# Second layer weights of six experts turned by DMA instead of TensorE in a macaron block on one Trainium2 core

## The reference

```python
def _swiglu(u, w1, w2, w3):                      # hidden size 341
    h = einsum('...d,hd->...h', u, w1); v = einsum('...d,hd->...h', u, w2)
    return einsum('...h,dh->...d', sigmoid(h) * h * v, w3)

def ffn(x):                                      # 8 routed experts, top 4, and a shared one
    gate = x @ Wg.T + routing_bias
    weights = softmax over the top 4 of gate, 0 elsewhere
    return _swiglu(x, Ws1, Ws2, Ws3) + sum_e weights[e] * _swiglu(x, W1[e], W2[e], W3[e])

x = x + 0.5 * ffn(layernorm(x))
x = x + attention(layernorm(x))                  # 16 heads of 64, causal, W_qkv and W_out
x = x + 0.5 * ffn(layernorm(x))                  # the same ffn weights
```

## Time and profile before

| | |
|---|---|
| median of three runs | 649.8 us |
| the profiled execution, in its own time | 649.4 us |
| its span, first to last instruction | 647.7 us |
| PE busy | 634.1 us (98%), 7870 products |
| DVE busy | 593.5 us (92%) |
| ACT busy | 562.2 us (87%) |
| POOL busy | 498.2 us (77%) |
| granted TensorE clock | 1.00 as the page lists it |
| chain that ended last | PE 88%, DVE 6%, issue 2%, ACT 2% |

### The profile page before, as it was taken

How to read it: one execution, slowest core, us unless ns; L and a number is a source line. 1 busy time by engine, 2 the same in 40 slices (tenths; PEclk the granted TensorE clock), 3 DMA queues, 4 the chain that set the end, 5 groups by cost and what they waited for, 6 DMA issues and landing times.

```text
span 647.7 us, 21027 instructions
## 1 busy us (share of the span) xinstructions
PE 634.1 (98%) x7870; PEld 419.4 (65%) x7870; DVE 593.5 (92%) x1655; ACT 562.2 (87%) x1108; POOL 498.2 (77%) x617
## 2 busy tenths in 40 slices
PE   6799999999999999999999999999999999999997
PEld 5466665666676566667657666756666676666666
DVE  4998799999999999999999999999999998888887
ACT  5989997999999799999889999998999996566554
POOL 3254785899899779799968988986799997665545
PEclk9999999999999999999999999999999999999999
DMA  7900000487789278796746777973698874200000
GB/s 202 285 2 2 3 1 2 84 146 133 129 123 169 42 124 140 126 136 120 128 70 122 140 137 127 148 132 63 107 137 147 140 138 78 50 18 2 18 1 18
DMA packets 226489, 62.97 MB, mean 97 GB/s; under 512 B 213202, under 2 KB 225620, under 8 KB 226388
## 3 DMA queue, kind: packets, MB, share of 16 engines
q1 hardware_dynamic: 226388, 61.64, 53.4%
HBM read 7.87 MB, written 1.05 MB: 14 GB/s over the span
## 4 chain that ended last, share of the span: by engine, by line
PE 88%; DVE 6%; issue 2%; ACT 2%; DMA 0%; POOL 0%; SPq 0%; DVEq 0%; POOLq 0%; ACTq 0%
PE bank L1164 25%; PE bank L1166 24%; PE bank L1165 24%; PE bank L1344 8%; PE bank L1307 5%; DVE probs L1842 2%; DVE glu L1750 1%; DVE xs L1781 1%; PE bank L1172 1%; DVE glu L1755 1%; PE bank L1208 1%; DMA bias_b<-in_L_ffn_routing_bias 0%; ACT gluh L1511 0%; ACT glu L1487 0%; POOL glul L1127 0%
## 5 line engine op out<-in xcount | busy, mean ns | idle before, releaser
L1127 POOL TENSOR_TENSOR glul<-glu,gluh 128x512 f16<-128x512 f32 x191 | 218.9, 1162 | 78.4 <-ACT gluh L1511 77.9
L1131 POOL TENSOR_TENSOR paired<-probs,paired 128x512 f16<-128x512 f32 x160 | 184.2, 1163 | 22.5 <-ACT paired L1536 21.6
L1490 ACT ACTIVATE glu<-bank,tanh_scale 128x512 f32<-128x512 f32 x167 | 112.4, 680 | 37.9 <-PE bank L1166 34.4
L1528 ACT ACTIVATE probs<-probs,exp_bias 128x128 f32<-128x128 f32 (+3 forms) x256 | 129.1, 552 | 4.2 <-POOL exp_bias L1139 4.1
L1842 DVE CUSTOM_DVE_ANT_0 probs<-bank,causal,score_scale 128x128 f32<-128x128 f32 (+3 forms) x256 | 126.2, 545 | 3.6 <-POOL paired L1131 2.9
L1164 PE MATMUL bank<-w3h,gluh 128*128 128x128 f16 x708 | 125.3, 219 | 0.1
L1166 PE MATMUL bank<-w3h,glul 128*128 128x128 f16 x708 | 125.1, 219 | 0.0
L1165 PE MATMUL bank<-w3l,gluh 128*128 128x128 f16 x708 | 125.1, 219 | 0.0
L1750 DVE SCALAR_TENSOR_TENSOR glu<-glu,bank 128x512 f32<-128x512 f32 x167 | 113.5, 679 | 9.6 <-ACT glu L1490 9.0
L1511 ACT ACTIVATE gluh<-glu 128x512 f16<-128x512 f32 x191 | 113.4, 623 | 9.6 <-DVE glu L1755 8.8
L1755 DVE SCALAR_TENSOR_TENSOR glu<-glu,bank 128x512 f32<-128x512 f32 x167 | 114.7, 687 | 5.8
(11 more groups left out here) (247 smaller groups left out, 1613.4 us busy)
## 6 DMA issues: line engine op xcount, KB each, us to landing
pT<-paired SPq DMA_TRANSPOSE x160, 3.3
attention_raw<-in_L_attn_W_qkv SPq DMA_DIRECT2D x6, 256.0 KB, 5.2
xs<-in_L_attn_inputs SPq DMA_DIRECT2D x4, 256.0 KB, 4.1
vh<-in_L_ffn_W SPq DMA_DIRECT2D x6, 128.0 KB
pT<-in_L_ffn_W SPq DMA_DIRECT2D x6, 128.0 KB
out<-xs SPq DMA_DIRECT2D x3, 256.0 KB, 2.8
raw_more<-in_L_ffn_W SPq DMA_DIRECT2D x4, 128.0 KB
attention_raw<-in_L_attn_W_out SPq DMA_DIRECT2D x2, 256.0 KB, 6.2
```

The lines of the kernel that those rows point to most:

```text
L1127: pool.tensor_tensor(glul[pair][:, :], g[:, :], gluh[pair][:, :], ALU.subtract).then_inc(glu_low)
L1131: pool.tensor_tensor(paired[n % PAIRED][:, 1, :], probs[n % PROBS][:, :], paired[n % PAIRED][:, 0, :], ALU.subtract).then_inc(probs_low)
L1490: act.activation(g[:, :], psum[b1.bank][:, :], ACT.Tanh, scale=tanh_scale[:, j:j + 1]).then_inc(tanh_made)
L1528: e = act.activation(pr[:, at:at + (qt + 1) * P], pr[:, at:at + (qt + 1) * P], ACT.Exp, bias=exp_bias[:, gp % 2, qt, head:head + 1], scale ...
```

## The change

w3 of the experts n = 3 to 8 no longer passes through TensorE and PSUM. POOL multiplies the raw weight by its scale in place (`scale_w3`), ACT copies it as float16 (`high_w3`), POOL subtracts (`low_w3`), both into `attn_pair`, a buffer that attention uses later, with the two halves of each part beside each other, and one DMA with transposition (`turn_w3`, on SP) brings both halves to their place; w3's high and low half are now two slices of one tensor for that. The step v of these experts only holds the bank that the transposition had, so that all others get the banks that they had. Products wait for the DMA (`drain_of`) instead of for DVE. `split_hidden`, `down` and all else are as before. Twelve unread products at the start become seven, five of which stand behind `norm_turn` and two behind the first `gate`. The order strings of all four engines are new; `Schedule` gives the same layers, shares and banks.

```diff
-WARMING = 12
+WARMING = 7
+TURNED_W3 = 3
@@ Schedule.turn_weights
-        if len(turned) == 3:
+        if len(turned) == (3 if n < TURNED_W3 else 2):
             self.raw_left[n] = use
@@ Schedule.prepare
+            if stage in "vr" and n >= TURNED_W3:
+                if stage == "v":
+                    self.spared[n] = self.free.popleft()
+                else:
+                    self.free.append(self.spared.pop(n))
+                    for kind in ("scale_w3", "high_w3", "low_w3", "turn_w3"):
+                        self.add(kind, n=n)
+                    self.weights_ready[n, 2] = TurnedW3(n)
+            elif stage in "tuv":
                 self.turn_weights(n, "tuv".index(stage))
@@ ORDER, two of its lines
-        "BFFFFFFFFFFFTTzFNTGTTSgNhhTGSTTTTThTddhhdhhGddShTTTddTdhhddTTdGhhShddTTTddTdhRhTdTXhhdzTdThhdTddghdh"
+        "BTzFFFFFTGNSgFFTTTNhhGSTTTTThdThdhhdhGddSTThTdddhhdTGddhdShhhTTTddddRhdThXddhzTTdhhhhdgddddhhhhhhhdd"
...
@@ macaron
-        w3h, w3l = sb("w3h", [P, len(PARTS), D], F16), sb("w3l", [P, len(PARTS), D], F16)
+        w3_pair = sb("w3", [P, len(PARTS), 2, D], F16)
+        w3h, w3l = w3_pair[:, :, 0, :], w3_pair[:, :, 1, :]
+        staged = lambda n: attn_pair[n % 2][:, :, :].rearrange("p a (j k) -> p (a j) k", k=D).rearrange("p (j a) k -> p j a k", a=2)[:, 0:len(TILES_OF[n])]
@@ sync
+                elif kind == "turn_w3":
+                    n = s["n"]
+                    q.wait_ge(w3_low, n - TURNED_W3 + 1)
+                    sp.dma_start_transpose(w3_pair[:, parts_of(n), :, :].rearrange("p j a d -> p (j a) d"),
+                                           staged(n).rearrange("p j a k -> p (j a k)")).then_inc(w3_turned[n % 2], 16)
@@ gpsimd
+                elif kind == "scale_w3":
+                    n = s["n"]
+                    raw = raw3[n % RAWS][:, 0:len(TILES_OF[n]) * P]
+                    q.wait_ge(scales_made, group_of(n) + 1)
+                    pool.tensor_scalar(raw, raw, scale_of(n, 4), None, ALU.mult).then_inc(w3_scaled)
+                elif kind == "low_w3":
+                    n = s["n"]
+                    raw = raw3[n % RAWS][:, 0:len(TILES_OF[n]) * P].rearrange("p (j k) -> p j k", k=P)
+                    q.wait_ge(w3_high, n - TURNED_W3 + 1)
+                    pool.tensor_tensor(staged(n)[:, :, 1, :], raw, staged(n)[:, :, 0, :], ALU.subtract).then_inc(w3_low)
@@ tensor, drain_of
+                if isinstance(use, TurnedW3):
+                    q.wait_ge(w3_turned[use.n % 2], 16 * ((use.n - TURNED_W3) // 2 + 1))
@@ scalar
+                elif kind == "high_w3":
+                    n = s["n"]
...
+                    q.wait_ge(w3_scaled, n - TURNED_W3 + 1)
+                    if n >= TURNED_W3 + 2:
+                        q.wait_ge(w3_turned[n % 2], 16 * ((n - TURNED_W3) // 2))
+                    act.activation(staged(n)[:, :, 0, :], raw, ACT.Copy).then_inc(w3_high)
```

More of the change, by code:

```diff
@@ L142 @@
 Turned = namedtuple("Turned", "n")
+TurnedW3 = namedtuple("TurnedW3", "n")
 class Schedule:
@@ new lines @@
+        "qkwwhwqwqhddwqhkwhwwxqxdqhhwwoqwwhdddwqqhwwhwhdwhdwhhwdwkwvvvwhxqxdvkhqqhddvhdkqdohwqqhvwwhwwqkdhwdq"
+        "qxghvwxwdwwqkdhdddwwqqhvhwwqkwhdwwdqqhhwwwxqxkhdwwqqhhddwwwqkdhdqqwwwhoqwhwddwqqhwwhxwhhxwdhdhwwdkwh"
+        "ddvvvvwwhqkhqqvhddxqxkhogwwhdwqqvhwddqwkhwwddqqhvhwwwqkhwddwqqhvwhwwxqxkhdwwqqhwdqwdwkhhwdwqqdwhwqkh"
+        "ddwwqqhwwxohwwqxhddwqqwhhddwwwhdhwhhwwdkvvwwhvvdqxghkxdqqhvhdddkqhowqqhdvwwhqwwkhwddqqxvwwhhwxqwkhwd"
+        "qqvdwhwwdwqkhddwqqhwhwwddqkhwwxqxqdwwhhwkqwhddwddqqwhhwoqwwdhqqwwhhdxwwwghhwxdddhhhddwwddwwhhhhhxhox"
@@ new lines @@
+        "rhsshhsshWhhssWsWsshhhWlWzhsskhsvvhvsvhshssskheeppsvehpeepkehppelhysvephpespkhseeppeuhspvehpeskpehpe"
+        "pusseevprhphsepepsskhepepusehpepkeheppesphsuepshepkheeppssuehphleypeephpusepespeshphhepsephhhsskssvv"
+        "vhusulvkheyepphssvhepeeppkehepspshevpheekpphepusseesprvhpseeppkhseupepshevphepepkhsseepsuphheepspekh"
+        "epupsephhespseekpephpuessphlepepyhepepsuehhpessphheepphhsssskhlyvvvuvhuskhepsehvpeeppkhssseeepprhpss"
+        "vehpepepkhepuessphevpheeppskheepsspuhevhpepepskheeppsuhespepepkhhespeupsehpseskphepepehuesplphysepep"
@@ new lines @@
+        "czhckhvvhvcvhhmkhmmvhmckhmmhvichmkhimcmhvihmkihmmgrvhjihcimkhmmchimkhimchmihmkhimnmhhicmaichmmihhich"
+        "hhnihkvvihvcmkhvmmhchvmckahmmhvihmkihmmgrjvchimikhcmmhvihmckhimmhihimkhcmmhhiimkcnhmmhcaimihnmmhhhci"
+        "ihhchikhcvvvivhmkhmmvhcmhkagrjhmmvihmickhmmhvichmkhimmhvhiimckhmmhciimkhhmmchimkhimnhminahmichmmchhi"
+        "ihchhhikvivhvvmgrjkhmmchvchmhkammhcivhmikhmmivhhcmikhmmcvhiimkhcmmnihhmkhimcmihhmikhcmmchhaimihmmhhi"
+        "iDDDDgrhjchhhiccihhhhhhahccnhhchhhhchhhhhccgrjhhhchhhhchchhhhchhhcchhhhhhccchhhhhHccclllllllllll"
@@ L893, in macaron @@
         first_gathered, first_spread = signal("first_gathered"), signal("first_spread")
+        w3_scaled, w3_high, w3_low = signal("w3_scaled"), signal("w3_high"), signal("w3_low")
+        w3_turned = [signal(f"w3_turned{i}") for i in range(2)]
         eps_made = signal("eps_made")
@@ L1154, in drain_of @@
             def drain_of(use):
-                q.wait_ge(drained[use.bank], use.n + use.d)
+                if isinstance(use, TurnedW3):
+                    q.wait_ge(w3_turned[use.n % 2], 16 * ((use.n - TURNED_W3) // 2 + 1))
+                else:
+                    q.wait_ge(drained[use.bank], use.n + use.d)
             def x_there(ready):
@@ L1398, in scalar @@
                     else:
-                        high_of(split, psum[split.use.bank][:, 0:len(TILES_OF[n]) * D],
-                                w3h[:, parts_of(n), :].rearrange("p j d -> p (j d)"), scale_of(n, 4))
+                        high_of(split, by_part(psum[split.use.bank], n),
+                                w3h[:, parts_of(n), :], scale_of(n, 4))
+                elif kind == "high_w3":
+                    n = s["n"]
+                    raw = raw3[n % RAWS][:, 0:len(TILES_OF[n]) * P].rearrange("p (j k) -> p j k", k=P)
+                    q.wait_ge(w3_scaled, n - TURNED_W3 + 1)
+                    if n >= TURNED_W3 + 2:
+                        q.wait_ge(w3_turned[n % 2], 16 * ((n - TURNED_W3) // 2))
+                    act.activation(staged(n)[:, :, 0, :], raw, ACT.Copy).then_inc(w3_high)
                 elif kind == "measure" and s["by"] == "A":
@@ L1661, in vector @@
                     else:
-                        high, low = (w[:, parts_of(n), :].rearrange("p j d -> p (j d)") for w in (w3h, w3l))
-                        low_of(split, psum[split.use.bank][:, 0:len(TILES_OF[n]) * D], high, low, scale_of(n, 4))
+                        high, low = (w[:, parts_of(n), :] for w in (w3h, w3l))
+                        low_of(split, by_part(psum[split.use.bank], n), high, low, scale_of(n, 4))
                 elif kind == "norm_stats":
```

47 lines of the change are left out of this document (16 added, 31 removed), and 2 rows, old and new, of the table KINDS.

## The result

The changed kernel takes 652.69 us (median of 12 runs, 650.99 to 654.76), the kernel before 649.84 (12 runs): ratio 1.0045, 95% interval 1.0034 to 1.0057. It is slower by 0.45%, 2.9 us; the forecast was 647.6 with a range up to 650.9. The profiled execution is the longest of the twelve (654.76 us, span 653.0), so its sizes are an upper end. The spread itself says something: the mean granted clock was 1.00 in three of the twelve runs, and these took 650.99, 651.13 and 651.59 us; it was 0.995 to 0.997 in seven (652.14 to 653.62) and 0.994 in two (654.63 and 654.76). So the kernel takes about 651.1 us at full clock, and the median lies 1.6 us above that, among runs with a lower clock.

What follows compares the result with a forecast made beforehand. PE bounds the first layer from 40 us, DVE and PE attention, PE the end. Gains of 2.0 us at the first projection, 0.2 from DVE's cushion, 0 behind: -2.2, median 647.6 us, range 645.9 to 650.9.

Steps and rivals of the forecast that it cites:

- The term for 18 to 40 us: Reordered `gather_max` and third silu free one copy's time before the tile at 26.09 us: gain 0.5 us, bounds 0 and 1.
- the port: Rival: small DVE steps of the scales blocked by POOL instructions, three more hits, 2.9 us less 0.5 slack: 650.0, chance 0.12.
- Half clock: Rival, at the start: native products at lower clock take 1.9 us longer; with POOL late 648.9 us, joint chance 0.12.
- Turnings, 2.2 us: First layer, PE: 20 w3 turnings removed at 0.11 us each; 17 lie in full PE time, gain 1.9 us.
- The start, +0.1 with bounds -0.5 and +1.9: Start: five unread products fewer bring nothing by themselves, since ACT's queue is late next; +0.1 us.
- POOL: Six subtractions 5.8 us and six scalings 5 us added; sum fits POOL's free time; arrives together with PE at first projection.
- The chain of POOL to the first projection: Before attention: last low half and 17 POOL instructions until 97.7 us, level with PE; taken as 98.0, gain 2.0.
- DVE and `expo`: Second router: `expo` 2.9 us earlier removes DVE's 3.55 us wait; DVE 2.2 us earlier at attention, counted as -0.2.
- DMAs and attention, 0: Six transposing w3 DMAs cost nothing, landing 3.3 us after issue; attention does the same work reordered, counted 0.
- The rival of the slower attention stage: Between 105 and 550 us the new order worsens DVE's queue, idle time above 17.1 us grows: 652.0 us, chance 0.18.

Runs made afterwards that it cites:

- splits_wait: Changed kernel, two groups of GpSimd low halves waiting for VectorE's scale_units, scaling of expert 3 put behind the first three low halves: 648.73 us, 0.9981 of the kernel before.
- warm12: Changed kernel with the five unread products put back at the head of TensorE's program, twelve instead of seven: 652.31 us, ratio 1.0029 to the kernel before.
- W3_alone: Kernel before, its orders and twelve unread products kept, only the w3 part for experts 3 to 8 changed, new operations placed by hand: 660.03 us, ratio 1.0156.

## Why the prediction was wrong, point by point

**The step that failed** is an overlap taken as free. The term for 18 to 40 us was a gain of 0.5, bounds 0 and 1, and POOL's additions between 40 and 60 us were free because "POOL is busy for 10.96 of 20". Both asked whether an engine has time, and neither asked what runs beside it. In their place the trace has PE gaps of 2.92 us (before 30.82) and 1.37 us (before 63.45) and a stretch of half clock behind each; all gaps of PE over 0.15 us from 24 to 70 us add up to 5.6 us, before to 0.9. The mechanism was in hand, as the rival called the port, from the earlier trace rows, and its price (three more hits, 2.9 us less 0.5 of slack) was nearly that of the first place alone (0.92 + 0.93 + 0.98 = 2.8 us over the times of before). It was given 0.12 because "it is one hit in four groups". That was a miscount in two ways. The trace before holds a second hit, a step of the scales on 15 columns at 50.87 us that takes 0.60 instead of 0.17. And the number of hits isn't a property of the chip that carries over, but of the two strings: the new one of DVE has `scale_units` ahead of two low halves, which the listings of the two orders tell without any run. In the trace after I count nine stretched small steps, 7.1 us in all over their normal time, against two with 1.4 us before. Seven of the nine stand beside low halves of tiles, which both kernels have; one, `spread` at 52.55 us with 0.98 instead of 0.22, beside a subtraction that the change added, and one beside an added scaling (0.47 instead of 0.24).

**Half clock** was the other rival that came true, at another place. It was expected at the native products, which took 2.40 us (the text named 2.5 as wrong), and cost 0.6 us at the start: with the data there at the same time (first turning at 7.42 and 7.45) the first low half is at 16.97 in splits_wait, with seven unread products, and at 16.39 in warm12, with twelve. In the changed kernel it is at 17.39, because the data landed 0.5 us later in this execution (first turning at 7.93). Behind the gaps at 27.9 and 62 us it cost more. At 2.4 GHz a product of 512 columns starts every 0.22 us, here every 0.42 us:

```profile
65.28 0.63 PE L1199 MATMUL bank<-xnT,w2h 128*128 128x512 f16 x1
65.70 0.63 PE L1200 MATMUL bank<-xnT,w2l 128*128 128x512 f16 x1
```

The clock of 0.83 on the mean of ten microseconds is 1.7 us of full clock lost in each of the two stretches. The profiled execution has two of them and lies 3.7 us over the 651.1 of full clock. The median lies 1.6 us over it, at 0.997, half of what that execution's 0.994 lacks, so it had one of them by that reckoning.

**Turnings, 2.2 us.** The number fits the bookkeeping. From 25 us on splits_wait has gaps of 0.61, 0.85, 0.59, 1.15 and 0.28 us, 3.5 in all, and the kernel before 0.24 and 0.67; yet at the 30th tile and at the last it is 0.2 us ahead, from 0.1 ahead at the second. So some 2.5 us of work are gone in between, near the 1.9 to 2.2 forecast (the two orders differ, so it is rough: at the 32nd tile it is 1.1 us behind). W3_alone won 1.3 to 1.7 us until it stalled. By itself the term is not shown.

**The start, +0.1 with bounds -0.5 and +1.9.** Measured +1.0 at the first low half and +0.3 at the second tile; inside the bounds. `spread0` came at 15.12 us, 1.1 later than worked out. ACT's queue was indeed what came late next (its first high half at 16.42, I had said 16.0).

**POOL.** The subtraction took 0.92 and 1.16 us, for 0.87 and 1.16. The scaling was mis-sized, outside my bounds of 0.52 and 1.16 for 512 columns:

```profile
L1105 POOL TENSOR_SCALAR paired<-paired,half_scale 128x384 f32<-128x384 f32 x2 | 2.5, 1253 | 16.1 <-DVE half_scale L1655 16.1
L1105 POOL TENSOR_SCALAR vl<-vl,half_scale 128x512 f32<-128x512 f32 x1 | 1.6, 1571 | 0.0
```

With one input tensor instead of two it is not shorter than the subtraction, but a third longer: 8.1 us for the six, where 5 were planned. The chain of POOL to the first projection did not decide: PE was full from 70 us on and got there at 107.07, 9 us behind the forecast of 98, with the last low half of n = 8 at 84.39. Since PE came so late, this is no test of how long POOL's chain is.

**DVE and `expo`.** ACT's table load for it is at 85.31 and `chosen` at 86.99, 8 to 9 us later than said, as everything is. DVE's wait of 3.55 us ahead of `chosen` is gone as said. But DVE is no busier there, 20.69 of 23.10 us where it was 22.17: it waits for PE now, which is late.

**DMAs and attention, 0.** Right: PE never waits for a `w3` DMA in the changed kernel, and attention's DVE idle time is 16.9 us. The rival of the slower attention stage, which had the whole chance of slower, 0.18, falls. That the kernel came out slower is no merit of it.

## What to carry to other kernels

When orders are drawn anew, look at what VectorE and GpSimd have beside each other, not at their busy shares. A VectorE step on a few columns of SBUF took 0.15 to 0.24 us alone and up to 1.2 us beside a GpSimd subtraction, and a chain of such steps paid once for each. An instruction added to GpSimd's queue can do harm from afar, by moving an old one upon such a chain. A wait that keeps the two apart can be worth more than it costs (here 4 us for two waits and one scaling moved). And count a gap of TensorE twice: for its length, and for the half clock that may follow. The sign of it here was that the runs spread with the granted clock (by almost 4 us, where the kernel before has 1.3, and 1.8 in its 25 runs).

## What the runs showed of the hardware

**Which VectorE operations stand still.** I went through the six traces (the kernel before, the changed one and the four experiments). The multiplications into `glu`, the collects and the low halves, which have one operand in PSUM, take the same beside a POOL instruction as without: 1604 multiplications `glu<-glu,bank` of 512 columns began beside one and none took more than 0.69 us, and of 1181 collects none took more than 0.35 us. Nor were layer norm statistics, reductions and reciprocals stretched, which read one tensor. Stretched were steps with two inputs in SBUF (`power`, `silu_scale`, and `chosen` in splits_wait, where both inputs lie in SBUF: 0.89 instead of 0.17 us), and steps with one input and a scalar, from SBUF to SBUF (`silu_back` 1.15 instead of 0.17, `spread` 1.22 instead of 0.22). Of both kinds 26 steps met a subtraction of POOL in the six traces, and each ended with it, within 0.05 us. The Trainium skill, SBUF — State Buffer, section Who interferes with whom, states both kinds: a VectorE instruction with two SBUF inputs contends with a GpSimd instruction that reads SBUF, and one in a two-port mode contends with GpSimd too, and who comes second is blocked for the whole instruction. The traces agree for POOL's subtractions, in all 26. The prediction had cited only the second half; the first is the one that makes `silu_scale`, three steps in a chain, so expensive.

**The new scalings did it seldom.** They read one tensor. In the changed kernel, while a scaling ran from 43.88 to 45.46 us, `silu_scale` took 0.47 us (0.24 alone), `unscale` 0.15 and the reciprocal 0.19, and none was held to its end. By the rule as the Trainium skill has it in the same section (a GpSimd instruction that reads SBUF) the steps with two inputs should have been. It does happen, though: of 24 small steps that began beside a scaling in the six traces (reciprocals left out) five took longer, to 0.47 or 0.51 us, and one of these, in warm12, ended with the scaling at 68.2 us:

```profile
66.61 1.57 POOL L1105 TENSOR_SCALAR vl<-vl,half_scale 128x512 f32<-128x512 f32 x1
...
67.70 0.51 DVE L1850 TENSOR_SCALAR w_max<-w_max 128x9 uint32<-128x9 uint32 x1
```

The same step took 0.17 us beside a scaling in two other traces; what decides is not shown. So the two gaps of PE come from low halves that are in both kernels, in new places, and the added instructions took part by their place in POOL's queue more than by what ran beside them (the step held by an added subtraction, at 52.55 us, has no gap of PE behind it).

**The clock falls behind gaps of different length, and not always.** It fell behind gaps of 2.92 and 1.37 us in the changed kernel; behind 1.90 us in the profiled execution of the kernel before it did not, and behind the same 1.90 us in the version with five unread products fewer it did. In warm12 a gap of 1.38 us had no fall behind it, and in the kernel with the w3 part alone it fell behind 2.56 us and not behind 1.60 and 2.78. So the length of the gap alone doesn't decide here. The Trainium skill, TensorE: Matmul & The Clock Gate, Part 1, says that an idle array is throttled and activity releases it; the trace agrees on that: behind the gap of 2.92 us products of 512 columns started every 0.42 us (33.05, 33.47) and a little later every 0.22 us again (34.24, 34.46).
